# Perceiver layer, one core: the opening's loads, splits and query spreading put in another order, with a Sqrt on ScalarE at the start

## The chip, the core and the metric

The kernel runs on one core of a Trainium2 chip. Its engines are PE (TensorE, matmuls; PEld is its weight load), DVE (VectorE), ACT (ScalarE), POOL (GpSimd) and SP (SyncE, which here issues DMAs); each works through its own instructions in order and waits on semaphores for the others. The metric is the device time of one execution in microseconds (us), the median of several.

## What is computed

Three residual layers on 128 rows of 256. The first, which fills nearly all of the time, is cross attention over a context of 12544 rows, with 16 heads of 16:

```python
x = x + xattn(layernorm(x), ctx, ctx, mask, Wq, bq, Wk, bk, Wv, bv)
x = x + attn(layernorm(x), Wqvk, Wo)
x = x + ffn(layernorm(x), w_gate, w_up, w_down)

def xattn(q, k, v, mask, Wq, bq, Wk, bk, Wv, bv):
    qh = (q @ Wq.T + bq).reshape(B, Sq, 16, 16)
    kh = (k @ Wk.T + bk).reshape(B, Sk, 16, 16)
    vh = (v @ Wv.T + bv).reshape(B, Sk, 16, 16)
    scores = einsum('bqhd,bkhd->bhqk', qh, kh) / sqrt(16)
    scores = where(mask[:, None], -1e7, scores)
    return einsum('bhqk,bkhd->bqhd', softmax(scores), vh)
```

Everything is float32. The mask of the inputs is empty; the kernel tests that at run time and takes one of two copies of its program.

## The kernel before

**First pass.** The context is cut into NB = 14 blocks of BK = 896 rows. For each block s, keys and values are projected, written to scratch in HBM, and rough scores are made only to find the row maxima. Each float32 operand of a projection is split into a high part (rounded, `ctx_hi`, `w_hi`) and a low part (`ctx_lo`, `w_lo`), and three products are summed (hi-hi, hi-lo, lo-hi), two chunks each: 6 matmuls for half a block of keys, 12 for two tiles of values. ACT casts the high parts (`high_piece`), POOL subtracts for the low parts (`split_context`, four pieces a block, `ctx_split` counts them). The order of PE's work in a block is the table `PROJECTIONS`: keys (half n of chunk m) and values (pair k) in turn, and after each, from `slots`, the scores of one group u, `score_for_max`. ACT evacuates each projection (L455, L461) and copies half of each group's scores (L468, L471); DVE makes the low part of the keys (`low_keys`, L627), takes maxima of the other half (L661) and folds the copies (L666), which lets POOL's next piece go (`run_taken`). Blocks 0 and 1 are written out by themselves, the others are a loop over two.

**The opening** is what comes before block 1. SP issues the loads in the order of L255 to L276 (L264, the mask, is the largest; L273 is block 1's context). The layernorm of x is DVE's alone (`layernorm`, with three Newton steps). PE transposes it (L905) and multiplies it with the query weights in their own layout (L912) for the rough scores (`q_pair`), and again with the query weights spread by ACT so that each pair of heads stands three times (L446 and L925, 8 groups times 2 chunks) for the exact ones; DVE adds the bias (L653) and writes `qr`, and POOL makes `q_stack` of it with two masks (L394 to L401, eight instructions). DVE reduces the whole mask for the flag (L643), PE sums it over partitions (L930). POOL halves the low part of block 0 with DVE (L383, L612) and fills `k_stack` with ones (L387).

**Second pass.** From about 241 us, per block, 8 groups of score matmuls (L996), of 6 and 8 head pairs in turn, each exponentiated by ACT from PSUM (L528) and then multiplied with the values (L1009). The loop runs 7 times over two blocks, so 16 exps (8 pairs) each. PE's order: scores of the next two groups, each when the exp before has left its PSUM banks, then the sums of the two before. What follows, to 489 us, are the second and third layer.

## Time and profile before

| | us |
|---|---|
| median of 3 runs | 490.97 |
| lowest, highest | 490.47, 493.65 |
| profiled execution | 491.17 |
| its span, first to last instruction | 489.5 |
| PE busy in the span | 467.0 (95%) |
| ACT busy | 379.3 (77%) |
| DVE busy | 283.7 (58%) |
| POOL busy | 101.9 (21%) |

All times of rows are counted from the start of the span. An engine's busy share says how full it is on average; what a change in a stage is worth shows in which wait ends last there, so the chain of waits and the timeline are the views to read next.

### The profile page before, as it was taken

How to read it: one execution, taken by the hardware profiler on the slowest of the kernel's cores; microseconds unless marked ns; L12 is line 12 of the kernel's file. 1: busy time of each engine (PE TensorE's matmuls, PEld its weight loads, DVE VectorE, ACT ScalarE, POOL GpSimd, SP SyncE). 2: the span in 40 equal slices, each digit the busy share in tenths (PEclk: the TensorE clock that was granted, in tenths of full speed). 3: DMA queues.
4: the chain of work that ended last, by engine and by line, in shares of the span. 5: the costliest groups of instructions: out<-in, count | busy, mean ns of one | idle time of the engine just before them, and what ended most of it. 6: DMA issues, size and time to landing. Idle time of an engine off the chain costs nothing.

```text
span 489.5 us, 16011 instructions
## 1 busy us (share of the span) xinstructions
PE 467.0 (95%) x6472; PEld 366.3 (75%) x6472; DVE 283.7 (58%) x409; ACT 379.3 (77%) x419; POOL 101.9 (21%) x102
## 2 busy tenths in 40 slices
PE   6999999999999999996999999999999999999797
PEld 3976777777777777763488899999999999976343
DVE  5779999999999999999649700000000000014585
ACT  4478888888888888876389899999999999973221
POOL 4696333333333333215000000000000000000000
PEclk9999999999999999998899999999999999999999
DMA  8895578765687656976957887777778877200000
GB/s 267 289 350 216 217 271 323 271 227 234 242 319 298 228 231 244 382 310 232 380 201 289 322 301 257 288 269 274 263 289 322 323 273 264 114 3 1 0 1 13
DMA packets 34762, 117.50 MB, mean 240 GB/s; under 512 B 4401, under 2 KB 10417, under 8 KB 34737
## 3 DMA queue, kind: packets, MB, share of 16 engines
q1 hardware_dynamic: 30560, 110.58, 59.5%
q0 software_dynamic: 4032, 6.42, 4.4%
q8 instruction: 19, 0.31, 0.2%
q10 hardware_dynamic: 144, 0.13, 0.1%
q14 instruction: 7, 0.05, 0.0%
HBM read 74.44 MB, written 39.47 MB: 233 GB/s over the span
## 4 chain that ended last, share of the span: by engine, by line
PE 72%; DVE 8%; ACT 7%; issue 6%; POOL 4%; DMA 1%; ACTq 0%; SPq 0%; POOLq 0%; DVEq 0%
PE ps_a L996 20%; PE ps_k L1009 19%; PE ps_a L852 11%; PE ps_k L843 10%; PE ps_a L886 6%; ACT early L471 4%; POOL k_stack L373 2%; DVE early L666 1%; DVE block_max L661 1%; DMA early<-in_ctx 1%; ACT k_stack L434 1%; POOL q_stack L401 1%; PE ps_a L897 1%; DVE early L697 1%; PE ps_a L925 1%
## 5 line engine op out<-in xcount | busy, mean ns | idle before, releaser
L661 DVE TENSOR_REDUCE block_max<-ps_a 128x2 f32<-128x896 f32 x112 | 121.3, 1083 | 0.3
L996 PEld LDWEIGHTS ps_a<-q_stack,k_stack 64*128 64x128 f32 x1568 | 96.2, 187 | 14.3 <-issue 12.6
L996 PE MATMUL ps_a<-q_stack,k_stack 64*128 64x128 f32 x1568 | 105.4, 279 | 0.9 <-DVE q_stack L707 0.4
L471 ACT CAST early<-ps_a 128x896 bf16<-128x896 f32 x104 | 93.9, 903 | 7.7 <-PE ps_a L886 7.7
L528 ACT ACTIVATE early<-ps_a 128x1536 f32<-128x1536 f32 (+1 forms) x56 | 90.1, 1663 | 8.8 <-PE ps_a L996 8.8
L528 ACT ACTIVATE middle<-ps_a 128x1536 f32<-128x1536 f32 (+1 forms) x56 | 90.2, 1662 | 7.2 <-PE ps_a L996 7.2
L729 DVE COPY early<-ps_k 128x256 f32<-128x256 f32 x2 | 0.8, 418 | 160.1 <-PE ps_k L1009 160.1
L852 PE MATMUL ps_a<-w_hi,k_stack 128*128 128x256 f32 x392 | 68.3, 297 | 0.0
L666 DVE TENSOR_TENSOR early<-early 128x896 bf16<-128x896 bf16 x104 | 64.6, 621 | 0.0
L843 PE MATMUL ps_k<-k_stack,w_hi 128*128 128x448 f32 x224 | 60.3, 391 | 2.9 <-DVE w_lo L616 1.6
L852 PEld LDWEIGHTS ps_a<-w_hi,k_stack 128*128 128x128 f32 x392 | 52.8, 189 | 11.7 <-issue 11.6
L886 PE MATMUL ps_a<-k_hi,q_pair 32*128 32x448 f32 x448 | 53.9, 470 | 7.9 <-ACT early L471 7.7
L843 PEld LDWEIGHTS ps_k<-k_stack,w_hi 128*128 128x128 f32 x224 | 37.7, 188 | 16.4 <-issue 13.9
L1009 PE MATMUL ps_k<-early,v_in 128*17 128x128 f32 x1568 | 49.1, 273 | 0.2
L1009 PE MATMUL ps_k<-middle,v_in 128*17 128x128 f32 x1568 | 49.0, 274 | 0.1
L461 ACT COPY early<-ps_a 128x512 f32<-128x512 f32 (+1 forms) x56 | 30.1, 537 | 24.0 <-PE ps_a L852 24.0
L886 PEld LDWEIGHTS ps_a<-k_hi,q_pair 32*128 32x128 f32 x448 | 21.8, 184 | 33.7 <-issue 22.7
L373 POOL TENSOR_TENSOR k_stack<-ctx_b,k_stack 128x448 fp32r<-128x448 f32 x28 | 32.0, 1146 | 64.2 <-DVE early L666 60.4
L455 ACT ACTIVATE k_hi<-ps_k,bk 128x448 fp32r<-128x448 f32 x56 | 35.6, 635 | 10.6 <-PE ps_k L843 9.4
L1009 PEld LDWEIGHTS ps_k<-early,v_in 128*17 128x17 f32 x1568 | 40.6, 97 | 2.9 <-issue 0.6
L1009 PEld LDWEIGHTS ps_k<-middle,v_in 128*17 128x17 f32 x1568 | 40.6, 97 | 2.6 <-issue 0.6
L423 POOL DMA_DIRECT2D mask_b<-in_maskt x12 | 6.3, 528 | 168.4 <-PE ps_a L996 168.4
(194 smaller groups left out, 471.1 us busy)
## 6 DMA issues: line engine op xcount, KB each, us to landing
k_stack<-k_hi_scratch SPq DMA_DIRECT2D x56, 448.0 KB, 6.0
v_scratch<-early SPq DMA_DIRECT2D x14, 952.0 KB, 5.9
v_in<-v_scratch SPq DMA_DIRECT2D x14, 952.0 KB, 7.8
k_hi_scratch<-k_hi SPq DMA_DIRECT2D x28, 448.0 KB, 3.1
k_lo_scratch<-k_lo SPq DMA_DIRECT2D x28, 448.0 KB, 3.6
k_stack<-k_lo_scratch SPq DMA_DIRECT2D x28, 448.0 KB, 6.1
early<-in_ctx SPq DMA_DIRECT2D x7, 896.0 KB, 7.6
ctx_b<-in_ctx SPq DMA_DIRECT2D x7, 896.0 KB, 7.7
```

Of the source, the lines that this page charges most:

```text
L373: nc.gpsimd.tensor_tensor(ctx_lo[:, par, c, half], ctx_bufs[par][:, c * BK:(c + 1) * BK][:, half], ctx_hi[:, par, c, half].bitcast(f32), A ...
L455: nc.scalar.activation(k_hi[:, par, m, n * HK:(n + 1) * HK], ps_k[:, 0:HK], ACT.Identity, bias=bk[:, m:m + 1]).then_inc(hi_ready, 1)
L461: nc.scalar.copy(v_new[:, par, tiles[0]:tiles[-1] + 1, :, 0:HD], ps_v[:, 0:len(tiles) * D].rearrange("p (t h d) -> p t h d", t=len(tiles), ...
L471: nc.scalar.copy(staged[:, u % 2], pair_scores(u, 0)).then_inc(max_copied, 1)
L528: nc.scalar.activation(probs[u % SLOTS_P][:, 0:width], ps_a[:, UNIT_BANK[u % 2]:UNIT_BANK[u % 2] + UP[u % 2] // 2, :].rearrange("p a n -> ...
L661: nc.vector.tensor_reduce(block_max[:, 2 * u:2 * u + 2, par], pair_scores(u, 1), AX.X, ALU.max).then_inc(max_taken, 1)
L666: nc.vector.tensor_tensor(copied_rows(u), copied_rows(u), staged[:, u % 2], ALU.max).then_inc(run_taken, 1)
L843: last = nc.tensor.matmul(ps_k[:, 0:HK], w[:, 0, c, m * P:(m + 1) * P], part[:, par, c, n * HK:(n + 1) * HK], start=(k == 0), stop=(k == l ...
L852: last = nc.tensor.matmul(ps_v[:, n * D:(n + 1) * D], part[:, par, c, t * P:(t + 1) * P], w[:, 1, c, :], start=(j == 0), stop=(j == len(te ...
L886: last = nc.tensor.matmul(outs[-1], q_pair[rows, head % 2, m, :], k_hi[rows, par, m, keys], start=True, stop=not masked, skip_group_check= ...
L996: last = nc.tensor.matmul(ps_a[:, base + bank, at * Q:(at + 1) * Q], k_stack[half, b_par, a, t * P:(t + 1) * P], q_stack[half, a, ab, :], ...
L1009: last = nc.tensor.matmul(attended[32 * j:32 * j + VW, c * Q:(c + 1) * Q], v_ring[:, b_par, t, h, :], probs[slot][:, col * Q:(col + 1) * Q ...
```

## The change

It changes how the work ahead of block 1 is laid out. The rest of the program stays, but for line numbers.

- SP asks for the key weights before the context, and for block 0's context and the mask in halves; the four loads of the spread bias `bqr` are gone, and block 1's context no longer waits for the mask.
- Block 0's low part is DVE's alone, four pieces of 448 columns. The first key projection waits for each operand by itself and stands ahead of the query matmuls. Three more projections follow before the queries are spread, and block 0's fourth key half (slot 8) comes ahead of the flag's branch.
- ACT adds the bias of the queries (`x3`). They are spread by 8 matmuls with an identity whose columns ACT repeats (`eye_4`), not by 16 with repeated weights; ACT copies the result to `qr`.
- The first layernorm takes its root from ACT, as the two others do. ACT begins with a Sqrt of a constant, so that the table is there.
- The mask's flag is reduced in two halves. POOL's fills of `k_stack` stand after its split of block 2; blocks 2 and 3 are written out of its loop.
- Fewer warming matmuls at the start: 9 for 12 and 2 for 6.

```diff
@@ SP
-            sp.dma_start(ctx_t, ctx_d[0]).then_inc(ctx_in[0], 16)
             sp.dma_start(w_kv[:, 0:DC * D], wk_d.rearrange("p c n -> p (c n)")).then_inc(wk_in, 16)
+            for n in range(2):
+                half = slice(n * HK, (n + 1) * HK)
+                sp.dma_start(ctx_t.rearrange("p (c k) -> p c k", c=DC)[:, :, half], ctx_d[0][:, :, half]).then_inc(first_in[n], 16)
...
-            for slot in range(STRIDE):
-                sp.dma_start(bqr[slot::STRIDE, :], bqr_d[0:2 * HD, :]).then_inc(rows_in, 16)
-                if slot:
-                    sp.dma_start(row_mask[slot::STRIDE, 0:2], pairmask_d[0:2 * HD, :]).then_inc(rows_in, 16)
+            for slot in range(1, STRIDE):
+                sp.dma_start(row_mask[slot::STRIDE, 0:2], pairmask_d[0:2 * HD, :]).then_inc(rows_in, 16)
             sp.dma_start(row_mask[SLOTS::STRIDE, 2:4], pairmask_d[0:2 * HD, :]).then_inc(rows_in, 16)
-            sp.wait_ge(mask_all_in, 16)
             sp.dma_start(ctx_bufs[1], ctx_d[1]).then_inc(ctx_in[1], 16)
@@ POOL
+            pool.wait_ge(mask_all_in[1], 16)
+            load_rows(0, 0, True)
+            load_rows(1, 1, True)
+            pool.wait_ge(ctx_split, PIECES)
+            split_context(1, 1, True)
+            pool.wait_ge(q_copied, 1)
+            pool.wait_ge(rows_ready, 1)
+            spread_queries(0)
+            spread_queries(1)
+            split_context(2, 0, False)
+            load_rows(2, 0, False)
+            for n, (fill, value) in enumerate(fills[-2:]):
+                nc.gpsimd.memset(fill, value).then_inc(consts_set, 1)
+                pool.wait_ge(consts_set, len(fills) - 1 + n)
+            split_context(3, 1, False)
+            load_rows(3, 1, False)
+            with pool.Fori(2, NB // 2) as i:
@@ ACT
+            act.wait_ge(consts_set, 6)
+            nc.scalar.activation(stats[:, 20:21], magic[:, 0:1], ACT.Sqrt)
+            act.wait_ge(eye_in, 16)
+            nc.scalar.copy(eye_4.rearrange("p (n s) -> p n s", s=STRIDE),
+                           eye[:, :].unsqueeze(2).to_broadcast([P, P, STRIDE])).then_inc(eye_spread, 1)
+            root(1)
+            high_weights(0, wk_in)
+            for n in range(PIECES):
+                act.wait_ge(first_in[n // 2], 16)
+                nc.scalar.copy(first_piece(ctx_hi[:, 0], n), first_piece(ctx_bufs[0].rearrange("p (c k) -> p c k", c=DC), n)
+                               ).then_inc(ctx_hi_ready, 1)
+            high_weights(1, wv_in)
...
+                        if first and work[1] == 1:
+                            high_piece(1, 1, 0)
+                            high_piece(1, 1, 1)
+                            act.wait_ge(q_projected, 2)
+                            nc.scalar.copy(qr.rearrange("p a q -> p (a q)"),
+                                           ps_a[:, 4:6, :].rearrange("p a n -> p (a n)")).then_inc(q_copied, 1)
+                            high_piece(1, 1, 2)
+                            high_piece(1, 1, 3)
@@ DVE
-            layernorm(x0[:]).then_inc(normed, 1)
+            layernorm_by_root(1, x0[:]).then_inc(normed, 1)
...
+            low_piece(0)
+            low_piece(1)
+            low_weights(0)
+            low_weights(1)
...
+            low_keys(0, 0, 0, 0)
+            low_piece(2)
+            low_piece(3)
...
+            ask_flag(0)
+            low_keys(0, 0, 0, 1)
+            ask_flag(1)
@@ PE
+            pe.wait_ge(w_high, 1)
+            project(0, 0, 0)
             pe.wait_ge(transposed_copied, 1)
...
             pe.wait_ge(w_split, 2)
             project(0, 0, 2)
+            pe.wait_ge(ctx_split, PIECES)
+            project(0, 0, 4)
+            project(0, 0, 6)
+
+            pe.wait_ge(x3_ready, DC)
+            pe.wait_ge(eye_spread, 1)
             for a in range(PR):
...
+                last = nc.tensor.matmul(ps_a[:, 4 + a // 4, (a % 4) * Q:(a % 4 + 1) * Q],
+                                        eye_4[:, (a % 4) * P:(a % 4 + 1) * P],
+                                        x3[:, (a // 4) * Q:(a // 4 + 1) * Q], start=True, stop=True)
```

What it makes of the programs is seen in the order of the built instructions. First ACT at the head of the second pass, before the change. The branch leads into the loop, whose body ends with the compare and branch (28 rows further on, not shown):

```order
L517 ACTIVATE q_stack<-ps_a 1x4x128 [waits max_rows_ready,q_spread]
L517 ACTIVATE q_stack<-ps_a 1x4x128 [waits max_rows_ready]
L522 UNCONDITIONAL_BRANCH [waits v_stored1,v_stored0]
L522 ISA
L528 ACTIVATE middle<-ps_a 128x1536 [waits prob_slots_free,scored]
```

The same place with the change:

```order
L543 ACTIVATE q_stack<-ps_a 1x4x128 [waits max_rows_ready,q_spread]
L543 ACTIVATE q_stack<-ps_a 1x4x128 [waits max_rows_ready]
L548 UNCONDITIONAL_BRANCH [waits v_stored1,v_stored0]
L548 ISA
L554 ACT_TABLE_LOAD [waits prob_slots_free]
L554 ACTIVATE middle<-ps_a 128x1536 [waits scored]
```

A table load stands ahead of the first exp of the loop's body, where none stood. The tables hold sets of functions; before, the first load of the program stayed good until the loop had ended.

PE in the opening, before, from the transposes of the normed x to the score group that follows the branch (ps_k holds keys, ps_a values, scores and queries; down_w is where the repeated weights, with the change the repeated identity, lie). Of each step the rows with a wait are shown:

```order
L905 MATMUL ps_a<-eye,xn 128x128 [waits eye_in,normed]
...
L912 MATMUL ps_a<-xt,wqn 128x128 [waits wqn_in,transposed_copied]
...
L843 MATMUL ps_k<-k_stack,w_hi 128x448 [waits w_split,low_context,ctx_split]
...
L852 MATMUL ps_a<-w_hi,k_stack 128x256 [waits w_split]
...
L925 MATMUL ps_a<-xt,down_w 128x128 [waits wq_spread]
...
L843 MATMUL ps_k<-k_stack,w_hi 128x448 [waits lo_ready]
...
L930 MATMUL ps_a<-ones_c,flag_f 1x1 [waits flag_asked]
L852 MATMUL ps_a<-w_hi,k_stack 128x256 [waits v_evacuated]
...
L934 TENSOR_LOAD flag_i [waits flag_ready]
...
L843 MATMUL ps_k<-k_stack,w_hi 128x448 [waits lo_ready,eyes_set,q_ready]
...
L886 MATMUL ps_a<-k_hi,q_pair 128x448 [waits hi_ready]
```

The same stretch with the change:

```order
L923 MATMUL ps_a<-eye,xn 128x128 [waits eye_in,normed]
...
L861 MATMUL ps_k<-k_stack,w_hi 128x448 [waits ctx_hi_ready,w_high]
...
L861 MATMUL ps_k<-k_stack,w_lo 128x448 [waits w_split] x2
L932 MATMUL ps_a<-xt,wqn 128x128 [waits wqn_in,transposed_copied]
...
L870 MATMUL ps_a<-w_hi,k_stack 128x256 [waits w_split]
...
L861 MATMUL ps_k<-k_stack,w_hi 128x448 [waits lo_ready,ctx_split]
...
L870 MATMUL ps_a<-w_hi,k_stack 128x256 [waits v_evacuated]
...
L944 MATMUL ps_a<-x,down_w 128x128 [waits eye_spread,x3_ready]
...
L950 MATMUL ps_a<-ones_c,flag_f 1x1 [waits flag_asked]
...
L861 MATMUL ps_k<-k_stack,w_hi 128x448 [waits lo_ready]
...
L955 TENSOR_LOAD flag_i [waits flag_ready]
...
L904 MATMUL ps_a<-k_hi,q_pair 128x448 [waits hi_ready,eyes_set,q_ready]
```

The first key projection stands ahead of the queries' and waits operand by operand, two more projections stand ahead of the spreading, and the branch comes one key projection later.

POOL between its small fills and its loop, with the change:

```order
L382 DMA mask_b<-in_maskn 128x896 [waits mask_all_in1,consts_set]
...
L375 TENSOR_TENSOR k_stack<-ctx_b,k_stack 128x448 [waits ctx_hi_ready,ctx_split]
...
L385 TENSOR_SCALAR q_stack<-v_in,row_mask 128x8x128 [waits rows_ready,q_copied]
...
L375 TENSOR_TENSOR k_stack<-early,k_stack 128x448 [waits run_taken,ctx_hi_ready,q_spread]
...
L382 DMA mask_b<-in_maskn 128x896 [waits max_scored,mask_in0]
L408 MEMSET k_stack 128x3584
...
L375 TENSOR_TENSOR k_stack<-ctx_b,k_stack 128x448 [waits run_taken,ctx_hi_ready,consts_set]
```

The two memsets of 128x3584 stood ahead of the first of these DMAs, behind the low half of block 0 (L383), which is gone from POOL.

## Rows read from the trace of the kernel before

**Rows 1.** The page's first part: busy us, share of the span, instructions by engine

```profile
PE 467.0 (95%) x6472; PEld 366.3 (75%) x6472; DVE 283.7 (58%) x409; ACT 379.3 (77%) x419; POOL 101.9 (21%) x102
```

**Rows 2.** Chain of waits of the first 60 us: start us, us, what

```profile
1.80 5.45 DMA early<-in_ctx
...
9.09 2.34 DVE k_stack L612
...
12.17 1.47 PE ps_k L843 x6
13.64 1.44 PE ps_a L852 x12
15.09 3.57 PE ps_a L925 x32
...
26.67 1.10 POOL q_stack L394
```

**Rows 3.** Timeline: start us, us, engine, line, operation; idle before, its releaser

```profile
22.87 0.48 PE L886 MATMUL ps_a<-k_hi,q_pair 32*128 32x448 f32 x4
...
24.90 0.48 PE L886 MATMUL ps_a<-k_hi,q_pair 32*128 32x448 f32 x4
...
28.71 1.08 PE L843 MATMUL ps_k<-k_stack,w_hi 128*128 128x448 f32 x4
...
43.04 1.14 POOL L373 TENSOR_TENSOR k_stack<-early,k_stack 128x448 fp32r<-128x448 f32 x1 [0.60 <-DVE early L666]
...
44.31 1.08 PE L843 MATMUL ps_k<-k_stack,w_hi 128*128 128x448 f32 x4 [0.59 <-POOL k_stack L373]
...
58.04 1.14 POOL L373 TENSOR_TENSOR k_stack<-ctx_b,k_stack 128x448 fp32r<-128x448 f32 x1 [2.69 <-DVE early L666]
```

**Rows 4.** Timeline of ACT in the second pass

```profile
241.73 3.22 ACT L528 ACTIVATE middle<-ps_a 128x1536 f32<-128x1536 f32 x2 [0.88 <-PE ps_a L996]
...
270.41 3.22 ACT L528 ACTIVATE middle<-ps_a 128x1536 f32<-128x1536 f32 x2 [0.67 <-PE ps_a L996]
274.47 3.22 ACT L528 ACTIVATE early<-ps_a 128x1536 f32<-128x1536 f32 x2 [0.84 <-PE ps_a L996]
...
298.66 3.22 ACT L528 ACTIVATE middle<-ps_a 128x1536 f32<-128x1536 f32 x2 [0.19 <-PE ps_a L996]
```

**Rows 5.** Timeline of ACT behind the second pass

```profile
437.08 1.28 ACT L537 ACT_TABLE_LOAD   x1
438.38 0.20 ACT L537 ACTIVATE stats<-magic 128x1 f32<-128x1 f32 x1
```

**Rows 6.** Timeline of PE in the second pass, two pairs of score groups

```profile
332.34 1.95 PE L996 MATMUL ps_a<-q_stack,k_stack 64*128 64x128 f32 x28
...
335.87 1.82 PE L996 MATMUL ps_a<-q_stack,k_stack 64*128 64x128 f32 x28
```

**Rows 7.** Busy by stretch: PE, PEld, DVE, ACT, POOL, granted clock, DMA, GB/s

```profile
6.00:8.00 2.00, 2.00 (x8) 1.00 (x7) 0.68 (x2) 0.72 (x1) 0.00 (x0) 1.00 1.02 384
```

**Rows 8.** ACT by line and form: count, busy us, mean ns, idle before, releaser

```profile
L455 ACT ACTIVATE k_hi<-ps_k,bk 128x448 fp32r<-128x448 f32 x56 | 35.6, 635 | 10.6 <-PE ps_k L843 9.4 <-PE ps_a L886 0.9
...
L434 ACT CAST k_stack<-early 128x448 fp32r<-128x448 f32 x24 | 13.8, 577 | 0.0
...
L468 ACT CAST early<-ps_a 128x896 bf16<-128x896 f32 x8 | 7.2, 904 | 0.3 <-PE ps_a L886 0.3
```

**Rows 9.** DVE by line and form, first 28 us

```profile
L643 DVE TENSOR_REDUCE flag_f<-middle 128x1 f32<-128x3136 int32 x1 | 3.4, 3400 | 0.0
...
L616 DVE TENSOR_TENSOR w_lo<-v_in,w_hi 128x512 fp32r<-128x512 f32 x2 | 1.3, 678 | 0.0
```

**Rows 10.** Timeline of POOL and SP in the opening

```profile
10.53 6.23 POOL L387 MEMSET k_stack<- 128x3584 f32 x2
...
14.30 0.58 SPq L273 DMA_DIRECT2D ctx_b<-in_ctx  x1
```

**Rows 11.** Instructions on the tile ctx_b from 14 to 22 us

```profile
DMA to landing us min/median/max: 4.9/4.9/4.9
```

More of the change, by code:

```diff
@@ L216, in perceiver_layer, with first_piece @@
         hidden_t = middle[:, 0:F].rearrange("p (t q) -> p t q", t=FT)
-        def wq_rows(c, first, end):
-            at, end = (c * PR + first) * P, (c * PR + end) * P
-            return down_w[:, at:end] if at < FT * D else wq_rest[:, at - FT * D:end - FT * D]
+        def first_piece(tile, n):
+            c, half = n % 2, slice(n // 2 * HK, (n // 2 + 1) * HK)
+            return tile[:, c, half]
         def group_heads(u):
@@ L426, in _, with root, high_weights @@
         def _(act):
-            def high_context(s, par):
-                act.wait_ge(ctx_in[par], (s - par) * 8 + 16)
-                nc.scalar.copy(ctx_hi[:, par].rearrange("p c k -> p (c k)"), ctx_bufs[par]).then_inc(ctx_hi_ready, PIECES)
             def high_piece(s, par, n):
                 c, half = n // 2, slice(n % 2 * HK, (n % 2 + 1) * HK)
-                act.wait_ge(ctx_in[par], (s - par) * 8 + 16)
+                act.wait_ge(ctx_in[par], s * 8 + par * 8)
                 nc.scalar.copy(ctx_hi[:, par, c, half], ctx_bufs[par][:, c * BK:(c + 1) * BK][:, half]).then_inc(ctx_hi_ready, 1)
-            act.wait_ge(ctx_in[0], 16)
-            nc.scalar.copy(ctx_hi[:, 0, 0, :], ctx_t[:, 0:BK]).then_inc(high_chunk, 1)
-            nc.scalar.copy(ctx_hi[:, 0, 1, :], ctx_t[:, BK:2 * BK]).then_inc(ctx_hi_ready, PIECES)
-            for part, arrived in enumerate((wk_in, wv_in)):
+            def root(nth):
+                act.wait_ge(variance_ready, nth)
+                nc.scalar.activation(small[:, 2:3], stats[:, 9:10], ACT.Sqrt, bias=magic[:, 2:3]).then_inc(root_ready, 1)
+            def high_weights(part, arrived):
                 act.wait_ge(arrived, 16)
@@ L530, in _ @@
                                          ACT.Exp).then_inc(exp_done, 1)
-            def root(nth):
-                act.wait_ge(variance_ready, nth)
-                nc.scalar.activation(small[:, 2:3], stats[:, 9:10], ACT.Sqrt, bias=magic[:, 2:3]).then_inc(root_ready, 1)
             nc.scalar.activation(stats[:, 20:21], magic[:, 0:1], ACT.Sqrt)
-            root(1)
+            root(2)
             nc.scalar.activation(stats[:, 21:22], magic[:, 1:2], ACT.Exp)
@@ L549, in _ @@
             nc.scalar.activation(stats[:, 22:23], magic[:, 0:1], ACT.Sqrt)
-            root(2)
+            root(3)
             nc.scalar.activation(stats[:, 23:24], magic[:, 0:1], ACT.Sigmoid)
@@ L951, in step @@
                     slots(s, par, range(0, H, 2))
-                slots(0, 0, range(H - 2 * LAG, H, 2))
+                score_for_max(0, 0, 0, masked)
+                slots(0, 0, range(H - 2 * LAG + 2, H, 2))
                 step(1, 1)
```

145 lines of the change are left out of this document (57 added, 88 removed).

## Prediction

> **What bounds the kernel now.** I read the page first: PE is busy 95% of the span, ACT 77%, POOL 21% [rows 1], so time is won or lost only where PE waits, or where an engine with little slack is given more. Two stretches matter.
>
> The opening. The chain of waits [rows 2] runs: block 0's context lands at 1.80 + 5.45 = 7.25, ACT casts it, DVE takes the low half in 2.34 and the low key weights, and only then does the first key projection start, at 12.17. PE then works almost without a hole, but 3.57 us of it, from 15.09, spread the queries. On the timeline [rows 3] PE scores block 0 from 22.87, starts block 1 at 28.71 and block 2 at 44.31, having waited 0.59 for POOL, whose last split of block 2 started at 43.04 after 0.60 of waiting for DVE. In the next block the last split starts at 58.04, 13.73 after the block. Later blocks keep that pace, so what the opening wins at 44.31 should arrive at the end.
>
> The second pass (about 241 to 437). ACT's exps run in pairs of 3.22 with, once settled, little idle between them, 0.19 before the pair at 298.66 [rows 4]. PE and ACT are both nearly full there, and ACT is the engine that gets an added instruction.
>
> **The table load in the exp loop.** The diff puts a Sqrt at ACT's start. The order shows the consequence: one table load more, the first instruction inside the loop over two blocks. The loop runs 7 times (eight pairs each), so 7 loads are added. The load after the loop starts at 437.08 with no idle before it, takes 1.28, and the next ACTIVATE starts at 438.38 [rows 5]. So I price a load at 1.28 + 0.03 = 1.31, serial on ACT.
>
> - First iteration: the first exp starts at 241.73 after 0.88 of idle, so ACT is free at 240.85 and would start at about 242.17: +0.45, all passed on to PE.
> - Second iteration (the pair at 270.41): 0.67 of idle stands before it and 0.84 before the next pair [rows 4]. Of 1.31 - 0.67 = 0.64 nearly all goes into the 0.84: +0.1 (0 to 0.6).
> - The other five: 0.19 of idle stands before the pair at a boundary, as at 298.66, so its exps come 1.31 - 0.19 = 1.12 late. PE has no room there. Its scores of two units take 1.95 in one pair and 1.82 in the next, and from one pair to the next it is 3.53 [rows 6]; the 0.13 more is PE waiting for an exp, since the 8-group scores reuse the bank that the previous exp reads. A late exp makes these scores late by all of it, less at most that 0.13. I take 1.02 each: 5.1.
>
> Sum of the loads: 0.45 + 0.1 + 5.1 = +5.65. Bounds: 0.45 if a reload of the set already active is free (no row shows such a reload), and 7 x 1.31 = 9.2 if no idle absorbs anything. I stay near the upper half since the rows of the load are of the same instruction on the same engine.
>
> The Trainium skill, "ScalarE: Activation LUTs", section "What ACT_TABLE_LOAD costs", gives 1283 ns for the load, as here, plus about 1380 ns of drain, some 2.66 us for every switch to another set. The rows at 437.08 and 438.38 show no such drain on either side, so the trace disagrees on that part. By the page's figure the seven loads would cost, as an estimate, some 15 us in place of 5.65.
>
> **The opening, step by step.** The stream moves 384 GB/s between 6 and 8 us [rows 7]. The first context half has 262 KB of key weights more ahead of it and 459 KB of context less in it than the whole had: 7.25 - 0.197/0.384 = 6.75. The second half has just the 262 KB more: 7.95. ACT: the high key weights are done before, casts of 448 columns at 0.58 [rows 8] end at 7.3, 7.9, 8.5, 9.1, high value weights 9.7. DVE: two low pieces at about 0.61 and the low key weights at 0.68 (both from the 0.68 of 512 columns [rows 9]): 9.3. The 2.34 for 896 columns [rows 2] stood beside a POOL subtraction, and POOL is idle there now; at half of 2.34 a piece the end would be 10.4. The layernorm by ACT's root ends sooner, which is hidden: its product waits for the query weights. PE ends the first key projection at 9.9, now 12.17 + 1.47 = 13.64.
>
> Then PE: query matmuls 1.1 (8 of the 32 that take 3.57 [rows 2], with their start) to 11.0, values 1.6, keys 1.4, values 1.6 (15.6), near the 1.44 and 1.47 of [rows 2]. The spreading has half the matmuls: 3.57/2 = 1.8 (17.4). The flag is hardly a wait: DVE's two halves of the 3.40 reduction [rows 9], with k_lo and the split between, end at 17.5. Keys again 1.4 and the flag's product: first scores at about 19.3 against 22.87, 3.6 earlier.
>
> Here ACT becomes the limit. It casts block 1's four pieces and now also copies the spread queries (DVE did) before it evacuates the next keys. Block 1's context is asked for at 12.1 in place of 14.30 [rows 10] (four small transfers fewer ahead, the two added issues fall where the queue is full) and takes the same 4.9 [rows 11] plus something for POOL's mask rows beside it: say 17.4. ACT [rows 8]: two pieces 18.55, the 1024-column copy about 1.04 (0.90 for 896) 19.6, two pieces 20.75, keys 0.64 21.4, score copy 0.90 22.3. PE's second scores wait for that copy: 22.3 against 24.90 [rows 3], 2.6 earlier, and block 1 starts at 26.2, 2.5 earlier. POOL splits block 1 behind the ACT pieces until 22.7 and then spreads the queries, which it starts at 26.67 now [rows 2]: 4.0 earlier. So it is ready for the last split of block 2 at 43.04 - 0.60 - 4.0 = 38.4, and DVE decides, at the pace of the next block: 26.2 + 13.73 = 39.9. With the split of 1.14 block 2 starts at 41.2: 3.1 earlier than 44.31, the 2.5 and the 0.6 that POOL and DVE held each other up.
>
> The fills, 6.23 on POOL [rows 10], move from before block 1 to after the split of block 2: 41.7 to 47.9. The last split of block 3 is wanted at 58.04 - 3.1 = 54.9; the 7.0 between hold the three other splits (3.4) with room. So the fills cost nothing; without the idle time that POOL has in each block they would cost up to 6.23.
>
> Opening: -3.1. Bounds: -1.3 if block 1's context lands as late as now (14.30 + 4.9 = 19.2, 1.8 after my 17.4), since ACT waits for it in order with the key evacuation behind; -3.9 if it lands at 16.5 and ACT's queue is no limit.
>
> **Sum.** The profiled execution is 491.17 (span 489.5): 491.17 - 3.1 + 5.65 = 493.7. It stands 0.2 above the median 490.97, so I give 493.5, +0.5%.
>
> **Rivals.**
> A (forecast), a load costs about 1.0 at a boundary and the opening wins 3.1: 493.5, own range 491.5 to 495.5, chance 0.73.
> B, a reload of the active set passes unseen; only the first load (0.45) is paid: 490.97 - 3.1 + 0.45 = 488.3. For it: no row shows such a reload. Against: nothing in the rows makes a load depend on what was active. 0.12.
> C, a load in mid-stream costs twice its 1.28, because ACT must also run empty around it: slower. Place: ACT between two iterations. With 2.57 + 0.03 the first iteration loses 2.60 - 0.88 = 1.7, the second about 1.3, the other five 2.60 - 0.19 - 0.1 = 2.3 each: 14.5, hence 490.97 - 3.1 + 14.5 = 502.4. It passes 1% from about 1.6 a load (seven times 0.34 more). Against it stand the rows at 437.08 and 438.38 [rows 5]. 0.04. The section of the Trainium skill named above is the page that speaks for it.
> D, ACT loses the opening: block 1's context lands at 19.2, the gain is 1.3, and the boundaries cost 1.2 each: 490.97 - 1.3 + 6.5 = 496.2. 0.08.
> The remaining 0.03: the opening wins over 5, with B.
>
> **Chances.** A measurement of this kernel tells from no change what lies beyond about 1%, 4.9 us. Faster (under 486.1): the last case, 0.03. Slower (over 495.9): C, most of D, the edge of A: 0.13. Within: 0.84. The range leaves out C, half of D, the last case and the edges: 488.0 to 495.9.
>
> **What would show it.** ACT_TABLE_LOAD 7 more times, 1.28 each, some 28 us apart, with about 1 us of PE idle behind each, and a second pass of about 201 in place of 196. First scores near 19.3, block 1 near 26.2, block 2 near 41.2. Wrong would be: loads with no late exp behind them, a fall of the granted clock in the opening, now 1.00 [rows 7], where PE works with holes from 7 to 10 us, or the last split of block 3 late behind the fills.

## The result and the profile after

| | median | executions | ratio to before |
|---|---|---|---|
| before | 491.98 us | 8, 490.47 to 493.73 | |
| after | 497.24 us | 8, 494.66 to 500.82 | 1.0117, interval 1.0091 to 1.0142 |

The change costs 1.2%, where 493.5 us and +0.5% were forecast, and 497.24 lies above the range of 488.0 to 495.9. The forecast was counted from a median of 490.97 us for before (3 executions); over eight it is 491.98, so 1.0 of the 3.7 us between 493.5 and 497.24 is no cost of the change. The profiled execution took 494.66 us (span 492.9), the least of the eight. The mean granted clock of the eight explains the order nearly whole: 0.989 and 0.990 in the three of 494.7 to 495.2 us, 0.983 at 496.9 and 498.1, 0.979 at 497.6, 0.976 at 498.5 and 500.8. Before's profiled execution had 0.993.

The page of after: the engines' busy time, the granted clock in 40 slices, and the scores of the second pass (busy us, mean ns, idle before them and its releaser).

```profile
PE 463.7 (94%) x6445; PEld 364.1 (74%) x6451; DVE 280.5 (57%) x404; ACT 389.0 (79%) x435; POOL 99.9 (20%) x101
...
PEclk9999999999999999997999998999999999999999
...
L1018 PE MATMUL ps_a<-q_stack,k_stack 64*128 64x128 f32 x1568 | 106.4, 280 | 6.3 <-ACT middle L554 5.9
```

ACT went from 379.3 to 389.0 us busy, PE's idle time before the scores from 0.9 us to 6.3, 5.9 of it released by an exp. The first 7 of the clock row is the dip that both kernels have at the end of the first pass (88 in before's row). New is the single 8 six slices on, at 296 to 308 us.

The opening, from the chain of waits (start, duration) and the timeline of PE:

```profile
12.62 4.91 DMA ctx_b<-in_ctx
...
19.39 0.47 PE L904 MATMUL ps_a<-k_hi,q_pair 32*128 32x448 f32 x4
...
21.90 0.48 PE L904 MATMUL ps_a<-k_hi,q_pair 32*128 32x448 f32 x4 [0.42 <-ACT early L480]
...
25.72 1.08 PE L861 MATMUL ps_k<-k_stack,w_hi 128*128 128x448 f32 x4
...
41.30 1.07 PE L861 MATMUL ps_k<-k_stack,w_hi 128*128 128x448 f32 x4 [0.59 <-POOL k_stack L375]
```

These rows answer to [rows 2, 3, 11]: first scores at 19.39 in place of 22.87, second at 21.90 for 24.90, block 1 at 25.72 for 28.71, block 2 at 41.30 for 44.31. POOL around the moved fills:

```profile
40.02 1.14 POOL L375 TENSOR_TENSOR k_stack<-early,k_stack 128x448 fp32r<-128x448 f32 x1 [2.16 <-DVE early L681]
...
41.71 6.27 POOL L408 MEMSET k_stack<- 128x3584 f32 x2
48.06 2.63 POOL L375 TENSOR_TENSOR k_stack<-ctx_b,k_stack 128x448 fp32r<-128x448 f32 x2
51.36 1.16 POOL L375 TENSOR_TENSOR k_stack<-ctx_b,k_stack 128x448 fp32r<-128x448 f32 x1 [0.66 <-DVE early L681]
55.11 1.14 POOL L375 TENSOR_TENSOR k_stack<-ctx_b,k_stack 128x448 fp32r<-128x448 f32 x1 [2.60 <-DVE early L681]
```

The second pass, ACT at three of the seven heads of the loop and behind it (against [rows 4, 5]):

```profile
237.84 1.28 ACT L554 ACT_TABLE_LOAD   x1
239.14 3.22 ACT L554 ACTIVATE middle<-ps_a 128x1536 f32<-128x1536 f32 x2
...
266.57 1.28 ACT L554 ACT_TABLE_LOAD   x1
267.86 3.22 ACT L554 ACTIVATE middle<-ps_a 128x1536 f32<-128x1536 f32 x2
...
295.29 1.28 ACT L554 ACT_TABLE_LOAD   x1
296.59 3.22 ACT L554 ACTIVATE middle<-ps_a 128x1536 f32<-128x1536 f32 x2
...
305.10 3.22 ACT L554 ACTIVATE middle<-ps_a 128x1536 f32<-128x1536 f32 x2 [2.18 <-PE ps_a L1018]
...
440.48 1.28 ACT L559 ACT_TABLE_LOAD   x1
```

The loop's start is 2.59 us earlier than before (239.14 against 241.73), its end 3.40 us later (440.48 against 437.08): it took 6.0 us more. One of the seven loads is followed by something that no other has, 2.18 us in which ACT waits for scores, before the pair at 305.10. PE there, and then the stretches (busy time of PE, PEld, DVE, ACT, POOL, then granted clock, DMA share, GB/s):

```profile
299.86 1.11 PE L1018 MATMUL ps_a<-q_stack,k_stack 64*128 64x128 f32 x16 [0.84 <-ACT middle L554]
300.90 3.03 PE L1031 MATMUL ps_k<-middle,v_in 128*17 128x128 f32 x56
303.86 2.08 PE L1018 MATMUL ps_a<-q_stack,k_stack 64*128 64x128 f32 x28
305.87 1.72 PE L1031 MATMUL ps_k<-early,v_in 128*17 128x128 f32 x56
```

```profile
299.00:300.00 1.00, 0.16 (x3) 0.14 (x4) 0.00 (x0) 1.00 (x2) 0.00 (x0) 1.00 0.98 387
301.00:302.00 1.00, 1.00 (x26) 0.91 (x28) 0.00 (x0) 1.00 (x2) 0.00 (x0) 0.56 1.01 405
302.00:303.00 1.00, 1.00 (x25) 0.91 (x20) 0.00 (x0) 0.92 (x1) 0.00 (x0) 0.50 1.09 445
...
305.00:306.00 1.00, 1.00 (x23) 0.93 (x25) 0.00 (x0) 0.91 (x1) 0.00 (x0) 1.00 0.24 99
```

PE stands still for 0.84 us, waiting for the late exp (busy 0.16 of the microsecond from 299). Such idle time of PE is called a hole in what follows. At 301.1 the granted clock falls from 1.00 to 0.50, from 2.4 to 1.2 GHz, for 3.4 us (called a fall); the 56 sums that take 1.72 us take 3.03, and ACT waits for what follows. The same hole stands at the head of every iteration, 0.81 us at the first and 0.84 at the six others, and in this profile only this one is followed by a fall.

### The profile page after: what moved, and what is told of

The parts are those of the page before. It is cut to its first block, busy times and chain, and to the rows that moved or that the text cites. A ratio compares the mean times of both kernels' runs of the same rounds, so it can differ in the third digit from the quotient of the medians.

```text
span 492.9 us, 15958 instructions
## 1 busy us (share of the span) xinstructions
PE 463.7 (94%) x6445; PEld 364.1 (74%) x6451; DVE 280.5 (57%) x404; ACT 389.0 (79%) x435; POOL 99.9 (20%) x101
## 4 chain that ended last, share of the span: by engine, by line
PE 67%; ACT 12%; issue 9%; DVE 7%; SPq 2%; DMA 1%; ACTq 0%; POOL 0%; DVEq 0%; POOLq 0%
PE ps_a L1018 16%; PE ps_k L1031 15%; PE ps_a L870 13%; PE ps_k L861 12%; PE ps_a L904 7%; ACT early L483 4%; ACT middle L554 4%; ACT k_stack L438 2%; DVE early L681 1%; DMA ctx_b<-in_ctx 1%; DVE block_max L676 1%; PE ps_a L915 1%; DVE early L712 1%; PE ps_a L1187 1%; DVE peak L787 1%
## 5 line engine op out<-in xcount | busy, mean ns | idle before, releaser
L642 DVE SCALAR_TENSOR_TENSOR k_lo<-ps_k,bk,k_hi 128x448 fp32r<-128x448 f32 x56 | 38.2, 683 | 7.0 <-ACT k_hi L467 4.1
```

What stands on the lines that cost most here:

```text
L642: nc.vector.scalar_tensor_tensor(k_lo[:, m, half], ps_k[:, 0:HK], bk[:, m:m + 1], k_hi[:, par, m, half].bitcast(f32), ALU.add, ALU.subtrac ...
```

## The experiments

Starts of the first exp in each iteration of the loop, read off ACT's timeline of the profiled execution, give the period of an iteration; the seven heads give six periods. All runs are compared with before, which was run again beside them (medians of 490.31 to 491.21 us), so the ratios compare across the experiments better than the medians. Everything that follows hangs on this table:

| kernel | periods of the loop's iterations, us | median, us |
|---|---|---|
| before | 28.68, 28.25, 27.72, 27.72, 27.71, 27.72 | 491.98 |
| after | 28.72, 28.73, **30.30**, 28.72, 28.72, 28.73 | 497.24 |
| no load in the loop (e4) | 27.71, 27.72, 27.72, 27.72, 27.72, 27.72 | 486.99 |
| the same once more (e11) | 28.04, 27.73, 27.72, 27.73, 27.72, 27.72 | 487.40 |
| loads kept, hole filled (e3) | 29.65, 28.73, 28.72, 28.73, 28.73, 28.72 | 493.82 |
| loads alone in before (e6) | 29.29, 28.72, 28.72, **30.30**, 28.71, 28.72 | 499.24 |
| activations as long as a load (e12) | 30.53, 28.58, 28.58, 28.58, 28.58, 28.58 | 493.69 |
| two loads (e7) | 30.40, 31.80, 34.86, 32.94, 31.83, 32.98 | 515.45 |
| two loads, hole filled (e14) | 31.51, 30.62, 30.24, 30.24, 30.24, 30.24 | 505.50 |
| activations as long as two loads (e13) | 31.82, 30.06, 34.66, 30.07, 34.72, 32.85 | 518.80 |

### Take the loads out of the loop

**e4**, the first layernorm's root back on DVE (Newton's steps), all else of the change kept:

```diff
-            layernorm_by_root(1, x0[:]).then_inc(normed, 1)
+            layernorm(x0[:]).then_inc(normed, 1)
...
-            nc.scalar.activation(stats[:, 20:21], magic[:, 0:1], ACT.Sqrt)
...
-            root(1)
```

> The changed kernel with the first layernorm's root back on the VectorE (Newton's steps, as before) in place of the Sqrt activation on ACT; with no Sqrt in the opening, the set of ACT at the loop is the one of Exp and no load stands in the loop. All else of the change is kept. Theory 1: 488.1 as with the Exp ahead of the loop; the norm is ready some 0.5 us later, which the first key projection, that needs no norm, covers. Theory 2 (the miss lies in the opening or the fills): 491.6. If the root on ACT is itself worth something in the opening, this run is slower than the one with Exp ahead of the loop by that, at most 1 us.

Measured 486.99 us (6 executions, 486.59 to 487.75), ratio 0.9927 (0.9899 to 0.9956): 1.1 us below theory 1, and 4.6 below theory 2. The same kernel once more:

> The kernel with no root on ACT once more, unchanged, beside the two others on one chip: 487.0 within 0.5, executions within 1.5 us, and a ratio to the kernel before of 0.992 to 0.994, which is the opening's gain of 3.1 us and up to 1 us for fewer falls of the clock.

487.40 us (10 executions, 486.50 to 490.04), ratio 0.9942 (0.9921 to 0.9963). So without the loads the change is a gain of 3 to 4 us, and this kernel beats both. Its ACT at the head of an iteration (timeline):

```profile
266.25 3.22 ACT L552 ACTIVATE middle<-ps_a 128x1536 f32<-128x1536 f32 x2 [0.30 <-PE ps_a L1030]
```

The 0.30 of idle before this pair is all that a load can hide in; the load and its gap take 1.30 (295.29 to 296.59 above), the difference is the 1.00 by which each period grows.

**e1**, the root stays on ACT, and a small Exp activation just ahead of the loop takes the load out of it:

```diff
+            nc.scalar.activation(stats[:, 21:22], magic[:, 1:2], ACT.Exp)
             for par in range(2):
                 act.wait_ge(v_stored[par], 16 * NB // 2)
             with act.Fori(0, NB // 2) as i:
```

> The changed kernel with one small Exp activation more on ACT, ahead of the loop of the second pass, where ACT waits for the last stores anyway; ACT_TABLE_LOAD then stands once ahead of the loop and no longer in its body, the computation is unchanged. Theory 1 (the seven loads cost their serial time, and the holes they leave on TensorE now and then cost granted clock too): all of the loss goes, and the opening's gain of 3.1 us is left: 491.2 - 3.1 = 488.1, mean granted clock 0.992 or more in every execution, spread as narrow as before's. Theory 2 (loads cost serial time only, the rest of the miss is somewhere else, in the opening or the later fills): the loads give back 5.65 us of 497.2, so about 491.6, and the mean clock stays below 0.99 in some executions. Theory 3 (the extra activation's load is late and moves the first exp): as theory 1 plus up to 1.3 us.

489.24 us (12 executions, 486.24 to 491.76), ratio 0.9969 (0.9942 to 0.9995), mean clocks from 0.993 down to 0.983: within theory 3, which is theory 1 and up to 1.3 us more. Timeline of ACT, and the stretches of 238 to 242 us:

```profile
238.54 1.28 ACT L546 ACT_TABLE_LOAD   x1
...
240.05 3.22 ACT L555 ACTIVATE middle<-ps_a 128x1536 f32<-128x1536 f32 x2
```

```profile
238.00:240.00 2.00, 1.69 (x24) 1.66 (x24) 0.78 (x2) 1.97 (x4) 0.00 (x0) 0.88 1.06 432
240.00:242.00 2.00, 2.00 (x11) 1.06 (x10) 0.00 (x0) 1.99 (x3) 0.00 (x0) 0.50 1.02 428
```

The load comes just behind the row copies that the first scores wait for, so the first exp is 1.5 us late once (240.05 against 238.54 in e4). The clock is at 0.50 from 239.5 to 243, but that is no fall behind the late exp, as the expectation of e5 takes it: it begins 0.5 us before the exp, and PE works from 238.31 to beyond 243 with scores and with matmuls of zeros that the kernel has there. It is also one fall of 3.4 us, not 6.8. **e5** puts the same activation ahead of the wait for the spread queries, into ACT's 6.8 us of idle at the end of the first pass:

> The changed kernel with the small Exp activation at the end of the first pass, ahead of the wait for the spread queries, where ACT stands still for 6.8 us; the load is then hidden whole, where in the run with Exp just ahead of the loop it moved the first exp by 1.5 us and TensorE's clock fell behind it (6.8 + 6.8 us at half speed in place of 6.8). Theory 1 (a late exp makes a hole on TensorE, and a hole now and then costs clock): 487.0, as the kernel with no root on ACT, executions within 1.5 us of each other. Theory 2 (the root on ACT in the opening is what makes the 2.2 us between the two kernels without loads in the loop): 489.2, as with Exp just ahead of the loop.

487.53 us (7 executions, 487.05 to 490.69), ratio 0.9939 (0.9915 to 0.9963), five of seven within 0.9 us and two at a mean clock of 0.983 and 3 us more. The median is theory 1's: the load of ACT's set is hidden, and the root on ACT does not cost 2.2 us.

The profiled execution is one of these two (490.43 us), and it shows what the profile of after does not: with the same opening, PE waits 1.92 us before the first key projection (at 8.26, in after 0.76 at 7.03), the clock falls for 3.4 us from 8.7 us and, behind a wait of 2.05 us, again from 22.4, and block 1 starts at 29.54, later than before's 28.71. So the opening's own gain is not the same in every execution. In the six profiles that have it, block 1 starts at 24.91 (e7), 25.71 (e3), 25.72 (after), 26.46 (e1), 27.44 (e14, also with a fall in the opening) and 29.54; in the three with before's opening it starts at 28.27 to 28.77.

### The loads alone

**e2** and **e6** are the kernel before with one small Sqrt activation, just ahead of the loop or in ACT's idle time at the end of the first pass, so that the loop gets its load and nothing else changes. The edit of e6; in e2 the line stands behind the copies, ahead of the waits for `v_stored`:

```diff
+            nc.scalar.activation(stats[:, 20:21], magic[:, 0:1], ACT.Sqrt)
             act.wait_ge(q_spread, 8)
```

> The kernel before with one small Sqrt activation more on ACT ahead of the loop of the second pass, so that the loop's body begins with a load of the Exp set in each of its 7 iterations, and nothing else of the change. Theory 1 (serial price and clock falls behind the holes): 491.5 + 5.65 + one to five falls of 1.6 us each, 499 to 505, with a median near 500 (the changed kernel's 497.2 plus the opening's 3.1), and executions that lie several us apart, the slower the lower their mean granted clock. Theory 2 (serial price alone): 497.1 in all executions, spread under 1 us more than before's, mean clock 0.993 less nothing.

502.40 us (6 executions, 498.47 to 504.87), ratio 1.0240 (1.0195 to 1.0286). Here two loads stand before the first exp, a fault of the place I had chosen; e6 is free of it.

> The kernel before with the small Sqrt activation at the end of the first pass, where ACT stands still for 6.8 us, so that the loop's body begins with a load in each of its 7 iterations and nothing else is late (in the run with Sqrt just ahead of the loop its own load and activation delayed the first exp by 1.5 us more). Theory 1: 491.0 + 5.65 + falls of the clock behind some of the holes (1.6 us each, one to four): 498 to 503, median 500, that is the changed kernel's 497.2 plus the opening's gain of 3.1. Theory 2 (serial price alone): 496.7, no fall in the loop. If it comes out at 497.2 or less, the opening of the changed kernel gives nothing.

499.24 us (6 executions, 497.04 to 501.72), ratio 1.0171 (1.0142 to 1.0199): 8.2 us for the loads alone, more than the 5.65 of serial price, and one period of 30.30 in the profile as after has, with the clock down behind a hole of 0.84 us. The mean clocks are 0.980 to 0.990, with before's opening, so the falls are not those of the new opening.

### Lateness or clock: fill the hole

**e3** is after with four matmuls of zeros at the head of the loop on PE:

```diff
+WARM_LOOP = 4
...
+                    for _ in range(WARM_LOOP):
+                        nc.tensor.matmul(attended, zeros_b[:, 0:P], zeros_b[:], start=False, stop=False, skip_group_check=True)
                     for u in range(0, 2 * UNITS, 2):
```

> The changed kernel with four matmuls of zeros more (about 0.22 us each, 0.86 us) at the head of each iteration of the second pass's loop, where TensorE waits about 1 us for the exp behind the load; the loads stay. Theory 1: TensorE no longer stands still there, the granted clock does not fall in the loop, and only the serial price is left: 491.5 - 3.1 + 5.65 = 494.0 in every execution (up to 0.5 more where the filler is longer than the hole), mean clock 0.99 and more. Theory 2 (serial price alone, and the spread has another cause): no change against 497.2, or up to 7 x 0.86 = 6 us more where the filler is on the path; the executions stay several us apart.

493.82 us (12 executions, 492.88 to 498.99), ratio 1.0064 (1.0030 to 1.0099), ten of the twelve within 1.9 us. Timeline of PE at a head:

```profile
268.76 1.72 PE L1032 MATMUL ps_k<-early,v_in 128*17 128x128 f32 x56
270.42 1.04 PE L1046 MATMUL ps_k<-zeros_b 128*128 128x512 bf16 x4
271.39 1.98 PE L1019 MATMUL ps_a<-q_stack,k_stack 64*128 64x128 f32 x28
```

PE goes from sums to zeros to scores without idle time, the late exp still sets the period (28.73), and no period has a fall in it. So 3.4 us of the median went with the hole and not with the load; by the ratios, each to before in its own set of runs, 1.0117 less 1.0064 makes 2.6 us. The mean clock says the same: it is on average 0.9895 here and 0.9832 in after, and that difference of some 495 us is 3.1 us. The opening is the same in both, so it does not make this difference. With the hole filled the change costs 0.64%, near the 0.5% that was forecast. Two executions kept a clock of 0.983 and 499 us; the profile, whose clock is down for 10.2 us at the end of the first pass in place of 6.8, shows only that falls outside the loop.

### The load itself or any late exp

**e9** and **e12** are e4 with six or fourteen small Exp activations at the head of the loop:

```diff
             with act.Fori(0, NB // 2) as i:
+                for k in range(14):
+                    small_work = nc.scalar.activation(stats[:, 24 + k:25 + k], magic[:, 1:2], ACT.Exp)
+                small_work.then_inc(spare, 1)
...
+                    if u == 4:
+                        act.wait_ge(spare, i + 1)
```

> The kernel with no root on ACT (no load in the loop, 487.0), with six small Exp activations (0.20 us each, 1.2 us) on ACT at the head of each iteration of the second pass's loop, in the place where the changed kernel has its load of 1.28 us. Theory 1 (a load costs nothing but its duration on ACT, which makes the exp late and leaves TensorE a hole): as the changed kernel, 487.0 + 7 x 0.9 = 493.4 and falls of the clock behind some holes, 1.6 us each, so 493 to 498, iteration periods 28.6 instead of 27.72 us. Theory 2 (a table load does something more to TensorE or to the clock than being late): 493.4 at most, with no fall in the loop, or less if the activations overlap the wait.

487.72 us (5 executions, 486.99 to 488.11), ratio 0.9935 (0.9913 to 0.9958). My size was wrong: six take 0.66 us together, not 1.2 (nor the 0.56 of the next expectation), and most of it fits into ACT's slack; the periods are 27.85 behind the first.

> The kernel with no root on ACT, with fourteen small Exp activations at the head of each iteration of the second pass's loop. In the run with six they took 0.56 us together (0.09 us each), half a load; the period of an iteration rose from 27.72 to 27.85 us and the time by 0.5 us. Fourteen should take 1.3 us, as one load with its gap (1.30 us from a load's start to the exp behind it). Theory 1 (a load costs only what makes the exp late, less the slack of ACT, and TensorE's hole then costs clock now and then): periods of 28.7 us, 487.2 + 6.4 = 493.6 plus falls of the clock, so a median of 494 to 498, and executions at different mean clocks. Theory 2 (the falls come of the load itself and not of the hole): 493.6 and the clock at 0.99 or more in all.

493.69 us (12 executions, 491.70 to 496.70), ratio 1.0047 (1.0022 to 1.0073). Timeline of ACT:

```profile
296.77 1.40 ACT L548 ACTIVATE stats<-magic 128x1 f32<-128x1 f32 x14
298.08 3.20 ACT L557 ACTIVATE middle<-ps_a 128x1536 f32<-128x1536 f32 x2
```

Periods of 28.58: lateness costs the same whoever causes it. On the clock the run speaks neither way clearly, and rather for theory 2. Its median is the 493.6 of the lateness alone, and its mean clocks (0.979 to 0.993, on average 0.988) lie between after's 0.983 and e3's 0.990. Its holes are 0.84 us at the first head, with a fall 1 us behind it (which may belong to the end of the first pass, as in e1), and 0.76 or 0.77 at the six later heads, with none. So for a hole of one load's length these runs show that filling it takes the falls away (e3), but not that the same hole without a load has as many. **e7** makes the hole larger, with a small Sqrt activation at the end of each iteration, hence two loads:

> The changed kernel with a small Sqrt activation at the end of each iteration of the second pass's loop: two loads (Sqrt, Exp) and the activation stand there, 1.28 + 0.20 + 1.28 us one behind the other, in place of one load. Serial price alone: 6 boundaries x 1.5 us more than the changed kernel, 497.2 + 9 = 506.2. Theory 1 (holes cost clock): the holes on TensorE are 2.5 us instead of 1, and behind more of them the clock falls: up to seven falls of 3.4 us at half speed, 1.7 us each, so 508 to 514, and a mean granted clock of 0.97 or less. A hidden price of a load beyond its own duration (a drain of 1.4 us) would show as gaps ahead of each of the two loads, and 10 us more.

515.45 us (4 executions, 513.42 to 518.66), ratio 1.0499 (1.0458 to 1.0540), clocks 0.957 to 0.967: theory 1, 1.5 us above its range. Clock row of the page, ACT and PE at a head:

```profile
PEclk9999999999999999979998988979999799899999
...
297.73 1.28 ACT L559 ACT_TABLE_LOAD   x1
299.02 0.20 ACT L559 ACTIVATE stats<-magic 128x1 f32<-128x1 f32 x1
299.24 1.28 ACT L556 ACT_TABLE_LOAD   x1
300.54 3.22 ACT L556 ACTIVATE middle<-ps_a 128x1536 f32<-128x1536 f32 x2
```

```profile
302.04 0.93 PE L1020 MATMUL ps_a<-q_stack,k_stack 64*128 64x128 f32 x12 [1.51 <-ACT middle L556]
303.81 1.97 PE L1020 MATMUL ps_a<-q_stack,k_stack 64*128 64x128 f32 x16 [0.84 <-ACT middle L556]
```

The clock falls behind each of the six later heads, for 3.4 us at three of them, 6.8 at two and 10.2 at one, where 3.4 each was expected. **e13** has thirty small activations in place of these two loads, **e14** keeps the two loads and gives PE ten matmuls of zeros:

> The kernel with no root on ACT, with thirty small Exp activations (2.8 us together) at the head of each iteration of the second pass's loop, as long as the two loads and the small activation between them (2.81 us from the first load to the exp). Theory 1 (the hole on TensorE costs the clock, whoever makes it): a fall in nearly every iteration, mean clock 0.955 to 0.97, and the time of the kernel with two loads, 515.4, less up to 1 us. Theory 2 (the table load costs it): no fall in the loop, clock 0.99, periods of 27.72 + 2.4 = 30.1 us, 487.2 + 7 x 2.4 = 504.0.

518.80 us (3 executions, 518.11 to 520.10), ratio 1.0575 (1.0531 to 1.0618), clocks 0.957 and 0.954, so 3.4 us above e7 where up to 1 below was expected; 2.5 of it stands ahead of the first exp (240.83 against 238.34), where e7 has one load only. The profile has falls in the first iteration and behind four of the six later heads, three of them of 6.8 or 10.2 us; the two periods of 30.06 and 30.07 are those without one.

```profile
PEclk9999999999999999968999987999879799899999
...
269.85 2.89 ACT L548 ACTIVATE stats<-magic 128x1 f32<-128x1 f32 x30
272.65 3.20 ACT L557 ACTIVATE middle<-ps_a 128x1536 f32<-128x1536 f32 x2
```

```profile
274.13 0.93 PE L1035 MATMUL ps_a<-q_stack,k_stack 64*128 64x128 f32 x12 [1.35 <-ACT middle L557]
```

> The kernel with two loads an iteration, with ten matmuls of zeros (0.21 us each, 2.1 us) at the head of each iteration on TensorE, where its hole of 1.5 + 0.8 us was. The loads stay. Theory 1: no fall in the loop or one or two at its start, mean clock 0.985 or more, periods of 30.1 to 30.3 us, 515.4 less seven falls of 1.6 us and more: 502 to 505. Theory 2: falls as before, 515 and clock 0.96.

505.50 us (3 executions, 503.99 to 507.76), ratio 1.0305 (1.0246 to 1.0364), clocks 0.983 to 0.990, at the edge of theory 1's 502 to 505. Clock row of its page: one dip in the opening, one at the end of the first pass as in every kernel here, none in the loop:

```profile
PEclk8999999999999999996999999999999999999999
```

For holes of two loads' length that settles the cause: with no load in the loop the clock falls nearly as often as with two, and with two loads and PE kept at work it does not fall there. The hole does it. For the hole of one load, which is the one of after, e3 and e6 carry the argument, and whether the load adds something of its own to it is open (e12).

### The fills

**e8** is e4 with Pool's two fills at the start of its program, where it is idle; **e10** the same with each fill cut into four.

```diff
+            for n, (fill, value) in enumerate(fills[-2:]):
+                nc.gpsimd.memset(fill, value).then_inc(consts_set, 1)
+                pool.wait_ge(consts_set, len(fills) - 1 + n)
             pool.wait_ge(mask_all_in[1], 16)
             load_rows(0, 0, True)
...
             load_rows(2, 0, False)
-            for n, (fill, value) in enumerate(fills[-2:]):
-                nc.gpsimd.memset(fill, value).then_inc(consts_set, 1)
-                pool.wait_ge(consts_set, len(fills) - 1 + n)
```

> The kernel with no root on ACT (no load in the loop), with Pool's two fills of 6.3 us moved from behind the third block's splits to the start of its program (2.6 to 8.9 us), where Pool waits for a transfer until 15.1 us. Theory 1 (the late fills cost nothing, since the splits of block 3 are on time behind them): no change, 487.0, within 0.5. Theory 2 (the fills beside DVE's low parts, 1.14 us each there instead of 0.8, hold DVE up at 41 to 48 us): up to 1 us faster, 486.0. Theory 3 (the fills beside the first layernorm on DVE at 5 to 9 us slow it and the first projection): up to 0.5 us slower.

490.63 us (12 executions, 489.85 to 492.74), ratio 0.9991 (0.9977 to 1.0006): 3.6 us slower than e4, 3.1 by the ratios, theory 3 in kind and six or seven times its size. Timeline of DVE, POOL and PE, and the stretch of 8 to 9 us:

```profile
5.80 3.20 DVE L610 TENSOR_SCALAR xn<-x,stats,small 128x256 f32<-128x256 f32 x1
```

```profile
2.63 6.23 POOL L397 MEMSET k_stack<- 128x3584 f32 x2
```

```profile
9.06 0.69 PE L935 MATMUL ps_a<-eye,xn 128*128 128x128 f32 x2 [4.17 <-DVE xn L610]
```

```profile
8.00:9.00 1.00, 0.00 (x0) 0.00 (x0) 1.00 (x1) 1.00 (x3) 0.86 (x1) 0.50 0.94 193
```

The last step of the layernorm, 0.41 us in e4, takes 3.20 us beside the fills and ends 0.14 us after them. PE, whose transposes wait for it in order ahead of the first key projection, stands for 4.17 us and then projects at half clock.

> The kernel with no root on ACT and Pool's fills at the start of its program, as in the run with the fills first (490.6), but each of the two fills of 128x1792 cut into four of 128x448 (0.8 us each). There the VectorE's last step of the first layernorm (128x256 from SBUF to SBUF, 0.41 us alone) took 3.20 us, from 5.80 us to the end of the second fill. Theory 1 (such a VectorE instruction waits for the end of the one Pool instruction that is under way): it takes 0.4 to 1.2 us, the first key projection starts at 7.3 to 8.0 instead of 10.0, and the time is 487.0 to 487.8. Theory 2 (it waits until Pool's queue has a pause): 3.2 us again, 490.6.

489.94 us (11 executions, 487.12 to 494.76), ratio 0.9984 (0.9969 to 1.0000). The profiled execution is the one of 494.76, so only its opening is read:

```profile
5.82 1.04 DVE L612 TENSOR_SCALAR xn<-x,stats,small 128x256 f32<-128x256 f32 x1
```

```profile
2.63 6.58 POOL L398 MEMSET k_stack<- 128x896 f32 x8
```

```profile
6.92 0.44 PE L937 MATMUL ps_a<-eye,xn 128*128 128x128 f32 x2 [2.00 <-DVE xn L612]
```

The step takes 1.04 us, 0.63 more than in e4 and less than the 0.82 of one piece, as theory 1 said. The time is not what it said: PE's wait of 2.00 us is still followed by a granted clock of 0.50 in the stretches from 8 to 14 us. Both places at the start cost 2 to 3 us against the one that the change gives the fills, behind block 2's split.

## Why the prediction was wrong, point by point

**The opening, -3.1: right in this profile and in the medians, not in every execution.** First scores 19.3 forecast, 19.39 measured; context of block 1 asked for at 12.1 and 12.62, landed at 17.4 and 17.53; second scores 22.3 and 21.90; block 1 26.2 and 25.72; block 2 41.2 and 41.30. The gain of 3.0 us reaches the end, as e4, e11 and e5 show with 4.0, 2.9 and 3.5 us in the medians. Rival D, by which block 1's context lands at 19.2, falls with it. But the prediction named a fall of the clock in the opening as a sign of being wrong. The profile of after has none, while those of e5 and e14 have, and e5's opening gains nothing at block 2 (44.60 against 44.31). Some of the spread between after's executions may come from there; the rows show one execution only.

**The fills, nothing: right.** Three splits of block 3 stand at 48.06 and 51.36, and the last starts at 55.11, where 54.9 was wanted, after 2.60 us of waiting for DVE. So POOL had room to spare behind the fills.

**The loads: the place and the mechanism right, the size in two parts wrong.** Seven loads of 1.28 us, each with a late exp behind it: rival B falls. The five later boundaries were priced at 1.02 each; 28.72 - 27.72 gives 1.00 for the last four. The first iteration's +0.45 is 0.4 (2.59 gained at the first exp of 3.0 at block 2). The second boundary, +0.1 because it had 0.67 of idle, is 0.04 in the two profiles (28.72 against 28.68), and the third, priced as the later ones, is 0.48 (28.73 against 28.25). But that idle was no property of the loop: e4 runs its first two iterations in 27.71 and 27.72 too (e11 in 28.04 and 27.73), so there also a load takes away up to 1.00 that the change could have kept. Against the kernel without loads the serial price is 0.4 + 6 x 1.00 = 6.4, not 5.65; e3 less the mean of e4, e5 and e11 is 493.8 - 487.3 = 6.5 (6.3 by the ratios).

**The failed step is the sum of the loads, which has no term for the granted clock.** The prediction saw "about 1 us of PE idle behind each" load, priced only the lateness in it, and looked for a fall of the clock only in the opening. In the loop a fall costs 30.30 - 28.72 = 1.58 us. One 3.4 us fall lowers the mean clock of such an execution by 0.0035, so the eight executions had, by their mean clocks, one to five falls more than before's profile. That is an estimate of their number, and not of their place. What the holes are worth at the median is the difference that e3 makes: 497.24 - 493.82 = 3.4 us, or 2.6 by the ratios. With that term the forecast of +0.5% becomes +1.0 to +1.2%, against +1.17% measured. Before has such falls too, but seldom more than one: of the 23 executions beside e1 to e4, ten had 0.993 (488.96 to 490.40 us), eleven 0.989 or 0.990 (490.88 to 493.41), two 0.983.

**The sum was made against one execution.** For the profiled one it would have been 493.7 with a measured 494.66, that is 1.58 for one fall, less 0.54 for the third boundary (28.25 before, so only 0.48 was lost there). The profile of after was one of the three of eight with the fewest falls, so even this agreement would have misled on the median.

**Rival C, a load that drains ACT as well: no.** In e7 the exp before ends at 297.71, and load, activation, load and exp follow at 297.73, 299.02, 299.24 and 300.54, with no gap over 0.02 us. The drain that the Trainium skill ("ScalarE: Activation LUTs", "What ACT_TABLE_LOAD costs") adds to a switch of sets does not appear in these rows; its 1283 ns for the load do. C's price of 2.6 us a boundary is not what made the time higher.

Left open: why a hole of 0.84 us is followed by a fall at one head and not at the five others; whether the fewer falls in e12 come of its slightly shorter holes (0.77 us) or of the missing load; and when the clock falls in the new opening. Only mean clocks over executions are known, and the place of a fall in one profile each.

## What to carry to other kernels

Ask of an edit what state it leaves behind for a loop far off: one Sqrt at the start of a program put a table load into every iteration of a loop 240 us later, and one small Exp activation in idle time, or no Sqrt, takes it out (487.0 to 487.5 us, the opening's gain kept). When something makes a full TensorE wait, price two things, the lateness and the clock that may fall behind the hole, and judge by the mean clock over many executions, since a single profile shows one draw. Where a wait can't be removed, matmuls of zeros in the hole give back the second part (3.4 us of the 9.9 between 497.24 and 487.3 here).

## What the hardware showed that I had not expected

- A hole of 0.84 us on TensorE in a stretch that is otherwise full was followed, 1.3 us after it ended, by 3.4 us at 1.2 GHz, at one of six heads of the loop with such a hole in this profile; with holes of 1.5 and 0.8 us close together it fell behind all six heads (e7), for 3.4 to 10.2 us.
- A VectorE instruction of 0.41 us, SBUF to SBUF, waited 2.8 us for the end of a POOL fill under way (e8), while the nine steps before it, 128x1 each, took the 0.14 to 0.28 us that they take in e4, though they stood beside the first fill. So did the statistics step, which reads 128x256 (0.43 us in both). With fills of 0.82 us it waited for one of them (e10). The Trainium skill says of the port pair that VectorE in some modes shares with GpSimd that it is "an exclusive lock, not a bandwidth split" ("SBUF — State Buffer", "SBUF: two separate sides"), held for a whole instruction; the two runs agree for this step. No run here tells which mode it ran in.
- A load of the set that was already active costs the same 1.28 us as a switch (the reload at 295.29 in after; the switches at 297.73 and 299.24 in e7).
